# A graph layer on one core: zeroing two edge-count tables without waiting for the small constants

## The chip, the cores and the metric

The kernel runs on one core of one Trainium2 chip. Its time is the device time of one execution in microseconds (us); a kernel is judged by the median of several executions. Engines are called PE (matrix multiply), DVE (vector), ACT (scalar), POOL (GpSimd) and SP (the queue that issues most loads and stores). Transfers that SP issues and transfers that POOL issues run on the same 16 DMA engines, in two queues that the profile calls q1 (hardware, SP's) and q0 (software, POOL's).

## The reference, cut to what matters

```python
# x: 1250 nodes x 768; src, dst: 21250 edges (20000 and one loop per node)
xn = layernorm(x)
# graph branch: its edges are src -> dst and one more loop per node
e     = leaky_relu(s_src[src] + s_dst[dst])
alpha = softmax of e over the edges of one dst
out   = segment_sum(alpha * h[src], dst)          # twice: 4 heads of 192, then 2 heads of 96
# mix branch: k, q, v = xn @ kqv_w.T + kqv_b; exp features of k and q by mix_w; linear attention; projection
x = x + gnn(xn) + mix(xn)
# then a layer norm, 8 experts with top-2 routing, and the last sum
x = x + ffn(layernorm(x))
```

The graph branch needs, for every pair (source, destination), how many edges join them. The kernel keeps this as a count matrix of 1280 x 1280 16-bit numbers in device memory.

## The kernel before

Nodes are laid out in ten tiles of 128 rows. Every engine has its own program, written out by hand; they meet at semaphores, so the order on each engine is the order in the code.

**The count tables.** Two tables in device memory, `table[0]` and `table[1]`, each 1280 x 1280 and a small spill area (3201 KB), are zeroed by POOL with one transfer each from a zero tile in on-chip memory (line 538). Then, for 28 chunks of 6 columns of 128 edges, DVE compares each edge's key with those of its neighbours (`compare_chunk`, line 922, operations at lines 929 to 939) and POOL adds the counts into the tables with 168 indirect transfers (line 549), three to each table per chunk. The first of them waits for the zeroing of its table, and each waits for the chunk's slots (`slots_done`). Much later POOL reads both tables back (`cnt`, lines 561 and 565).

**POOL's start.** POOL fills the zero tile and some constants with memsets, waits until DVE has copied the transposed edge keys out of a PSUM bank (`keyT`), writes them to `key_d` with two transfers (lines 530 and 531), and then comes to the zeroing.

**SP's start.** In this order: the edges, x in tiles 0 to 5, half 0 of the k weights (`w_raw`, line 410), x tiles 6 to 9, then 31 small constants that all count on the semaphore `consts_in`: `kqb_c`; `gb_c` in two transfers of 4-byte pieces, 1536 in all (line 419); three rows of 3 KB broadcast to 128 partitions (`accb`, `row_t`, `row_b`, line 422); 24 pieces of `mix_w` of 64 partitions x 128 bytes (lines 426 and 428); the router weights (`rw_raw`, line 429, last, 768 pieces of 32 bytes). After them come half 1 of the k weights (line 410), the v weights (`whole`, line 408, 768 pieces of 3 KB) and the edge keys broadcast to all partitions (`keyrow`, line 438).

**Who waits for the constants.** `N_CONST` is 31, and four engines wait for all of them: PE ahead of its first k product (line 1321), ACT after it has cast half 1 of the k weights (line 640), DVE after it has split x (line 919), and POOL ahead of the zeroing (line 535).

**The stage around them.** DVE takes the mean and variance of x tile by tile (`tile_stats`, lines 876 to 880), normalises tiles 0 to 4 and then 5 to 9 (line 914); PE transposes each half (line 1291); ACT and DVE split the transposed halves into high and low parts. PE then runs 18 k groups in a row (`K_MAIN`, line 1280), and ACT evacuates each (lines 647 and 648). After the eleventh (`j == 10`) ACT takes a square root (`root(3)`, line 629) for which DVE waits after its first two compare chunks (line 869); only then does DVE do the other 26 chunks, and PE's first product over the values waits until they are done.

Of the kernel before, what the change touches and what calls it, by code (L numbers as in the profile page):

```python
# [22 lines left out]
def gps_layer(nc, x, src, dst, norm_g, norm_b, W1, a_src1, a_dst1, b1, W2, a_src2, a_dst2, b2, Wu, bu,  # L23
# [12 lines left out]
    H2, C2 = a_src2.shape  # L36
    MH, HD, M = mix_w.shape
    E, _, FI = w1T.shape
    GR = src.shape[1]
    KW = 3  # L40
# [15 lines left out]
    with ctx:  # L56
# [143 lines left out]
        def sem(name):  # L200
            return ctx.enter_context(nc.semaphore(name))
# [3 lines left out]
        consts_in, edges_in, rows_in = sem("consts_in"), sem("edges_in"), sem("rows_in")  # L205
# [187 lines left out]
        N_CONST = 7 + 2 * MH  # L393
# [111 lines left out]
        def _(pool):  # L505
# [26 lines left out]


            pool.wait_ge(zero_done, 1)
            pool.wait_ge(consts_in, 16 * N_CONST)
            for i, tab in enumerate(table):
                view = tab.rearrange("(p a n) o -> p a (n o)", p=P, n=ZW)
                pool.dma_start(view, zero[:, :].unsqueeze(1).broadcast_to([P, view.shape[1], ZW])).then_inc(table_zeroed[i], 16)
# [1092 lines left out]
```

## Time and profile before

| what | value |
|---|---|
| median of 3 runs | 1316.11 us (1314.32 to 1346.6) |
| the profiled execution's own time | 1314.55 us |
| its span, first to last instruction | 1312.8 us |
| PE, DVE, ACT, POOL busy | 83%, 62%, 31%, 23% of the span |
| chain that ended last, by engine | PE 60%, DVE 26%, issue 7%, DMA 3% |
| mean granted clock of PE | 0.916 |

Work in the profile is told by engine, line of the kernel and operands (out<-in). The chain that ended last is followed back from the last instruction; time outside it costs nothing by itself. Times within the execution are microseconds from the start of the span.

### The profile page before, as it was taken

Reading aid. Unit: us, or ns where it says so; the run is one execution under the profiler, and the core shown is the slowest. Engines: PE = TensorE matmul, PEld = TensorE weight load, DVE = VectorE, ACT = ScalarE, POOL = GpSimd, SP = SyncE. Lnnn points to the kernel's source line nnn. Section 1 sums busy time; section 2 is a strip of 40 time slices with the busy share of each in tenths; the row PEclk is TensorE's granted clock in tenths of the full one; section 3 lists DMA queues with packets and bytes.
Section 4 is the critical chain, followed back from the end, with each engine's and each line's share of the span. In section 5 each row is a group of like instructions: output and inputs, shape, how many; then the busy total and the mean of one; then the engine's idle time right before and its main releaser. Section 6 shows DMA issues by size and latency. Waiting matters only on the chain.

```text
span 1312.8 us, 15580 instructions
## 1 busy us (share of the span) xinstructions
PE 1092.2 (83%) x6105; PEld 975.1 (74%) x6105; DVE 816.8 (62%) x1648; ACT 401.0 (31%) x522; POOL 306.4 (23%) x227
## 2 busy tenths in 40 slices
PE   2999956999999992018999794678699999999998
PEld 1898535667899992018888794677569999999998
DVE  7558993107632595978999668697935433454344
ACT  2443010334100214017666331672242221222211
POOL 1157888888883400010000000000000000000000
PEclk8999985999999996558999897798899999999999
DMA  6926652423555804012000002001010111011103
GB/s 205 312 47 157 127 102 14 72 1 50 118 117 57 238 18 138 0 41 81 1 1 0 1 22 99 0 1 49 1 48 1 48 48 49 1 48 49 49 0 118
DMA packets 67241, 83.14 MB, mean 63 GB/s; under 512 B 31419, under 2 KB 50189, under 8 KB 67169
## 3 DMA queue, kind: packets, MB, share of 16 engines
q1 hardware_dynamic: 37601, 62.27, 15.2%
q0 software_dynamic: 29568, 19.89, 10.1%
q8 instruction: 48, 0.79, 0.3%
q14 instruction: 24, 0.20, 0.0%
HBM read 67.59 MB, written 14.54 MB: 63 GB/s over the span
## 4 chain that ended last, share of the span: by engine, by line
PE 60%; DVE 26%; issue 7%; DMA 3%; ACT 3%; POOL 1%; DVEq 0%; SPq 0%; ACTq 0%; POOLq 0%
PE bank L1280 51%; PE bank L1482 7%; DVE junk_m L1060 7%; DVE junk_k L929 6%; DVE pbuf L1131 3%; DVE pbuf L1105 3%; PE bank L1291 2%; ACT vbuf L762 1%; DVE h L1114 1%; DMA cnt<-table 1%; DVE sb_stats L876 1%; DVE x L1180 1%; DVE sb_stats L877 1%; ACT pbuf L771 1%; DMA keyrow<-key_d 1%
## 5 line engine op out<-in xcount | busy, mean ns | idle before, releaser
L549 POOL DMA_INDIRECT table<-match_n,slot_ix x168 | 277.6, 1652 | 89.6 <-issue 49.7
L1482 PE MATMUL bank<-h,pbuf 128*128 128x193 f32 (+1 forms) x1200 | 190.2, 319 | 31.5 <-DVE pbuf L1131 30.4
L1482 PEld LDWEIGHTS bank<-h,pbuf 128*128 128x128 f32 x1200 | 181.6, 197 | 40.1 <-DVE pbuf L1131 35.9
L1280 PE MATMUL bank<-f_hi,hT 128*128 128x384 f32 x640 | 167.4, 336 | 0.0
L1280 PEld LDWEIGHTS bank<-f_hi,hT 128*128 128x128 f32 x640 | 117.0, 189 | 0.6
L1211 DVE TENSOR_TENSOR hT<-silu,hT 128x512 fp32r<-128x512 f32 (+1 forms) x48 | 28.8, 603 | 141.4 <-ACT hT L825 141.3
L1262 DVE SCALAR_TENSOR_TENSOR x<-bank,sb_gate,x 128x384 f32<-128x384 f32 x160 | 93.5, 613 | 28.9 <-PE bank L1280 28.6
L1280 PE MATMUL bank<-f_lo,hT 128*128 128x384 f32 x320 | 107.7, 337 | 0.0
L1280 PE MATMUL bank<-y2T_hi,f_hi 128*128 128x512 f32 (+1 forms) x288 | 103.2, 358 | 2.9 <-DVE y2T_lo L860 2.9
L929 DVE SCALAR_TENSOR_TENSOR junk_k<-keyrow,key,sb_before 128x384 uint8<-128x384 f32 x168 | 92.8, 614 | 20.1 <-DMA keyrow<-key_d 20.1
L1280 PE MATMUL bank<-y2T_lo,f_hi 128*128 128x512 f32 (+1 forms) x288 | 102.9, 357 | 0.0
L1280 PE MATMUL bank<-y2T_hi,f_lo 128*128 128x512 f32 (+1 forms) x288 | 102.9, 357 | 0.0
L1060 DVE CUSTOM_DVE_ANT_0 junk_m<-a_row,pen 128x1280 bf16<-128x1280 f32 x60 | 89.5, 1492 | 21.1 <-DMA a_row<-s_d 12.2
L823 ACT ACTIVATE silu<-bank 128x512 f32<-128x512 f32 (+1 forms) x48 | 25.4, 528 | 244.9 <-PE bank L1280 244.9
L771 ACT ACTIVATE pbuf<-pbuf 128x1280 f32<-128x1280 f32 x60 | 76.1, 1269 | 58.3 <-DVE pbuf L1105 58.3
L1131 DVE SCALAR_TENSOR_TENSOR pbuf<-pbuf,cnt 128x1280 f32<-128x1280 f32 x60 | 88.7, 1484 | 0.0
L1280 PE MATMUL bank<-xnT_hi,w_hi 128*128 128x512 f32 (+1 forms) x216 | 84.4, 391 | 0.9 <-ACT qpT L674 0.9
L1280 PE MATMUL bank<-w_hi,xnT_hi 128*128 128x384 f32 x240 | 81.2, 338 | 0.0
L1280 PE MATMUL bank<-w_hi,xnT_lo 128*128 128x384 f32 x240 | 80.7, 336 | 0.0
L1280 PE MATMUL bank<-w_lo,xnT_hi 128*128 128x384 f32 x240 | 80.6, 336 | 0.0
L1280 PE MATMUL bank<-xnT_lo,w_hi 128*128 128x512 f32 (+1 forms) x216 | 77.8, 360 | 0.0
L1280 PE MATMUL bank<-xnT_hi,w_lo 128*128 128x512 f32 (+1 forms) x216 | 77.6, 359 | 0.0
(244 smaller groups left out, 1992.3 us busy)
## 6 DMA issues: line engine op xcount, KB each, us to landing
keyrow<-key_d SPq DMA_DIRECT2D x28, 384.0 KB
table<-zero POOLq DMA_DIRECT2D x2, 3201.0 KB, 28.4
cnt<-table POOLq DMA_DIRECT2D x20, 320.0 KB, 10.9
f_raw<-in_w1T SPq DMA_DIRECT2D x8, 768.0 KB, 4.8
f_raw<-in_w2T SPq DMA_DIRECT2D x8, 768.0 KB, 6.3
w_raw<-in_kqvT SPq DMA_DIRECT2D x4, 1152.0 KB, 7.1
acc_d<-ubuf SPq DMA_DIRECT2D x20, 192.0 KB, 2.1
u_row<-m_d POOLq DMA_DIRECT2D x6, 640.0 KB, 7.8
```

The costliest lines, as they stand in the source:

```text
L549: pool.indirect_dma_start(table[i], bass.IndirectOffsetOnAxis(ap=slot_ix[:, g:g + 1], axis=0), match_n[:, g:g + 1], None, compute_op=ALU.a ...
L771: nc.scalar.activation(pbuf[i % 3][:, :], pbuf[i % 3][:, :], ACT.Exp).then_inc(e_done, 1)
L823: nc.scalar.activation(sbuf[g % 3][:, 0:w], b[:, 0:w], ACT.Silu).then_inc(free("H", e, c, m), 1)
L929: nc.vector.scalar_tensor_tensor(out=junk_k[g % 2][:, :], in0=keyrow[c % KR][:, w:w + KW * P], scalar=key[:, g:g + 1], in1=before[:, first ...
L1060: ins = nc.vector.tensor_tensor_reduce(out=junk_m[:, :], in0=rows_a[h][:, :], in1=pen_t[:, :], scale=1.0, scalar=-3e38, op0=ALU.subtract, ...
L1105: nc.vector.scalar_tensor_tensor(out=pbuf[i % 3][:, :], in0=u1_r[h][:, :], scalar=scol[:, h, st:st + 1], in1=vbuf[i % 2][:, :], op0=ALU.ad ...
L1131: nc.vector.scalar_tensor_tensor(out=pbuf[i % 3][:, :], in0=pbuf[i % 3][:, :], scalar=2.0, in1=cnt[st][:, :], op0=ALU.min, op1=ALU.mult).t ...
L1211: nc.vector.tensor_tensor(hT[j % 2][1][:, g % 2, 0:w], sbuf[g % 3][:, 0:w], hT[j % 2][0][:, g % 2, 0:w].bitcast(F32), ALU.subtract).then_i ...
L1262: nc.vector.scalar_tensor_tensor(out=a, in0=b[:, 0:HALF], scalar=gate[:, t, e:e + 1], in1=a, op0=ALU.mult, op1=ALU.add).then_inc(free("O", ...
L1280: return nc.tensor.matmul(o, l, r, start=first, stop=last)
L1291: ins = nc.tensor.transpose(b[0:channels, j * P:(j + 1) * P], piece(j), ident[:, :])
L1482: ins = nc.tensor.matmul(b[:, d * stride:d * stride + chans + 1], score[:, dt * P:(dt + 1) * P], h_t[:, st, h, 0:chans + 1], start=st == 0 ...
```

## The change

One wait is taken out of POOL's program. The zeroing of the two tables then waits only for the zero tile; the two key transfers still stand ahead of it, and every reader of the tables keeps its wait.

```diff
@@ -532,7 +532,6 @@
             pool.wait_ge(zero_done, 1)
-            pool.wait_ge(consts_in, 16 * N_CONST)
             for i, tab in enumerate(table):
                 view = tab.rearrange("(p a n) o -> p a (n o)", p=P, n=ZW)
                 pool.dma_start(view, zero[:, :].unsqueeze(1).broadcast_to([P, view.shape[1], ZW])).then_inc(table_zeroed[i], 16)
```

No instruction changes its place on any engine. POOL's list around the zeroing, with what each instruction waits for, was this before (`key_d` is the key scratch, `zero` the zero tile):

```order
L530 DMA key_d<-keyT 128x128 [waits bank_free0,consts_done]
L531 DMA key_d<-keyT 40x128
L538 DMA table<-zero 1536x1x1067 [waits consts_in,zero_done]
L538 DMA table<-zero 1536x1x1067
L549 DMA table<-match_n,slot_ix 1638912x1 [waits table_zeroed0,slots_done]
```

and is this with the change (the lines behind it are numbered one less):

```order
L530 DMA key_d<-keyT 128x128 [waits bank_free0,consts_done]
L531 DMA key_d<-keyT 40x128
L537 DMA table<-zero 1536x1x1067 [waits zero_done]
L537 DMA table<-zero 1536x1x1067
L548 DMA table<-match_n,slot_ix 1638912x1 [waits table_zeroed0,slots_done]
```

The zeroing follows the key transfers at once, and nothing else moves.

## Rows read from the trace of the kernel before

**Rows 1.** The chain of waits in order of time: start us, us, what.

```profile
38.72 23.34 PE bank L1280 x125
...
91.99 0.69 ACT kq L647
...
94.65 0.22 ACT sb_sq L629
...
96.05 3.34 DVE junk_k L929 x12
```

**Rows 2.** Who waited for whom, whole span: us in total, times, longest us.

```profile
POOL table L538 <- DMA sb_rw_raw<-in_routerT: 27.7, 1, 27.7
...
POOL cnt L561 <- DMA acc_d<-ubuf: 25.7, 1, 25.7
...
DVE junk_k L929 <- DMA keyrow<-key_d: 20.1, 4, 15.3
...
DVE sb_rs L869 <- ACT sb_sq L629: 14.4, 4, 13.6
```

**Rows 3.** Timeline of POOL: start us, us, engine, line, operation, idle before it.

```profile
8.33 0.58 POOL L531 DMA_DIRECT2D key_d<-keyT  x1
36.64 2.05 POOL L538 DMA_DIRECT2D table<-zero  x2 [27.74 <-DMA sb_rw_raw<-in_routerT]
```

**Rows 4.** Timeline of SP's DMA queue: start us, us taken to issue.

```profile
9.81 4.29 SPq L419 DMA_DIRECT2D sb_gb_c<-in_norm_b  x1
14.13 2.59 SPq L422 DMA_DIRECT2D sb_accb<-in_bu  x1
...
18.56 0.55 SPq L426 DMA_DIRECT2D sb_wk<-in_mix_w  x1
...
33.87 0.59 SPq L429 DMA_DIRECT2D sb_rw_raw<-in_routerT  x1
34.50 0.55 SPq L410 DMA_DIRECT2D w_raw<-in_kqvT  x1
```

**Rows 5.** DMA issues by line: KB each, median us from issue to landing.

```profile
sb_rw_raw<-in_routerT SPq DMA_DIRECT2D x1, 24.0 KB, 2.2
```

**Rows 6.** Timeline of DVE, PE and ACT, one row of each.

```profile
28.70 0.56 DVE L876 BATCH_NORM_STATS2 sb_stats<-xrow 128x6 f32<-128x384 f32 x1
...
38.51 0.47 PE L1280 MATMUL bank<-xnT_hi,w_hi 128*128 128x512 f32 x1
...
40.70 2.13 ACT L601 ACTIVATE w_hi<-w_raw 128x2304 fp32r<-128x2304 f32 x1 [1.40 <-DMA w_raw<-in_kqvT]
```

**Rows 7.** DMA packets of 0 to 13.6 us, all queues, by size.

```profile
DMA packets 2057, 3.98 MB, mean 293 GB/s; under 512 B 177, under 2 KB 1213, under 8 KB 2057
```

**Rows 8.** DMA queues, 13.6 to 23 us: packets, MB, share of 16 engines.

```profile
q1 hardware_dynamic: 3072, 2.63, 99.4%
```

**Rows 9.** DMA queues, 36 to 41 us (no row of q0 there).

```profile
q1 hardware_dynamic: 899, 1.57, 96.4%
```

**Rows 10.** DMA queues, 42 to 57 us.

```profile
q0 software_dynamic: 770, 3.25, 58.2%
q1 hardware_dynamic: 798, 2.35, 44.2%
```

**Rows 11.** DMA queues, 60 to 63 us.

```profile
q0 software_dynamic: 215, 0.92, 102.9%
```

**Rows 12.** DMA queues, 63 to 66 us.

```profile
q0 software_dynamic: 137, 0.58, 105.6%
```

**Rows 13.** DMA queues, 113.5 to 118.5 us.

```profile
q1 hardware_dynamic: 622, 1.83, 98.6%
q0 software_dynamic: 515, 0.00, 16.1%
```

**Rows 14.** Stretches: us, busy time of each engine (instructions), PEclk, DMA share, GB/s.

```profile
24.60:32.20 7.60, 0.00 (x0) 0.00 (x0) 6.84 (x21) 2.00 (x2) 0.00 (x0) 0.50 0.09 14
32.20:38.20 6.00, 6.00 (x27) 5.63 (x28) 6.00 (x8) 4.16 (x9) 1.56 (x2) 0.50 0.49 115
```

## The prediction, made before the changed kernel had run

> **What bounds the kernel now.** I read the chain of waits first, then the list of waits, then the timelines of the queues around the edit, and last what the DMA queues moved.
>
> The chain says who sets the pace at the start. PE enters it with the k products at 38.7 us; it leads through PE's work to ACT's evacuation at 91.99 and the square root at 94.65, and hands over to DVE's compare chunks at 96.05, on which the next PE stage hangs [rows 1]. So a shift of the first k product is a shift of everything behind it, and a shift of DVE's first two chunks alone is not: after them DVE stood 13.6 us waiting for that square root [rows 2].
>
> The count tables are off this chain. POOL waited 27.7 us for the last constant before it zeroed [rows 2, 3], but after its last scatter it stood 25.7 us waiting for something else [rows 2]. POOL's scatters of chunks 2 to 27 need DVE's slots, which come only after 96 us [rows 1]. Zeroing earlier by itself therefore buys nothing.
>
> **What the change does, part by part.**
>
> *The wait.* The issue of the zeroing moves from 36.64 to just behind the key transfer that ends at 8.91 [rows 3], 27.7 us earlier. Before, no packet of q0 moved from 36 to 41 [rows 9]; by 42 to 57 they ran at full rate [rows 10]. That is 4.4 to 5.4 us from issue to the first packet; I take 4.7, so zeros begin to move at about 13.6.
>
> *What they meet there.* 2057 packets had moved by 13.6, 1213 of them under 2 KB [rows 7]. The other 844, less 16 of the keys, are rows of x, so of its 1280 rows about 450 are still to come. Behind them in SP's queue stand 1664 small pieces (`kqb_c` 128, `gb_c` 1536), 384 rows of 3 KB, 24 pieces of `mix_w` and the router weights. Before, SP's queue had the engines alone: 3072 packets from 13.6 to 23 at 99.4% [rows 8]. After that they were nearly idle while SP issued its small transfers, and that is the gap that invites the change.
>
> *How the two queues share.* From 42 to 57 q0 moved 770 packets of zeros and q1 798 of loads [rows 10], one for one, 51 pairs a us. The zeros are some 1540 packets (two tables of 3201 KB, at the 4.2 KB a packet of this row). Do small pieces pair one for one too? The nearest rows: at 113.5 to 118.5, 2-byte scatter packets and 3 KB loads ran 515 to 622 [rows 13]. I take one for one, as these rows are near to it.
>
> *The sum for the constants.* (1) 450 x rows at 51 pairs a us: 8.8 us, so x is in at about 22.4. DVE needs the last tile at 28.70 [rows 6]; covered, with 6 us left, and without that cover a late tile would push DVE, then PE's transposes, one for one. (2) The 1090 zeros left pair with the small pieces at the rate of zeros alone: 215 in 3 us, 72 a us [rows 11], gives 15.1 us, to 37.5. At the slower rate of the row behind it, 46 a us [rows 12], it would be 23.7 us, to 46. (3) SP cannot run far ahead of its queue: the second transfer of `gb_c` took 4.29 us to issue and the next 2.59, against 0.55 to 0.59 once the queue had drained [rows 4]. When the 4.29 ended, the packets issued and not moved were 450 less those of half a us, and 1664: some 2000 to 2100, and I take 2048 as what fits. Three rows then go out as x drains, by 22; after that each `mix_w` transfer of 64 pieces waits for 64 to drain. 1090 drained pieces let 17 of the 25 last transfers out by 37.5. The 8 left take 0.64 us each (25 in the 15.9 us from 18.56 to 34.50 [rows 4]), 5.1 us, to 42.6, and the last lands 2.2 us after its issue begins [rows 5]: about 44. The 384 rows (1.2 MB) need some 3.5 us of the same stretch and are hidden in it.
>
> *What hangs on it.* PE starts its k products at 44 and not at 38.51 [rows 6]: **+5.5 us**. POOL's other user of the semaphore is gone; DVE's sum at line 920 waits too, but its next work, the first compare chunk, waits for `keyrow` anyway (15.3 us before [rows 2]). ACT's cast of half 1, issued 0.6 us behind the last constant, moves from 40.70 to about 49; its product is used after two k groups, some 8.5 us after 44, so it just fits. `keyrow` lands behind it and the v weights, at about 56 (57.8 before), with 13.6 us and more of cover.
>
> *PE's clock.* PE had no work from 24.6 to 32.2 and its granted clock was 0.50, the 1.2 GHz level; it stayed there for 6 us of work, to 38.2 [rows 14]. With the change PE stands from 38.5 to 44; no row shows an idle stretch of just that length, so it may fall again or not. If it is low for the first 5 us or so of the k products, they lose half of these: **+2.5 us**, between 0 and 3; I take the fall, since the stretch that is shown is the nearest.
>
> *The other side of the ledger.* From 42 to 72 the loads no longer share with zeros. What they feed there is `keyrow`, whose wait lies under the 13.6 us: 0. The scatters lose their wait for the second table (3 us of POOL): 0 under the 25.7.
>
> Sum: 5.5 + 2.5 = **+8 us** on the profiled execution's 1314.55, 1322.6. The median stands 1.6 above that execution, and it is of three runs with one far off; I say **1323 us**.
>
> **The Trainium skill against this.** The Trainium skill, "DMA: Bandwidth & Descriptors", section on queues, rings and completion order, says that each DMA engine alternates between queues by packets, and that such a packet is typically 9 to 17 descriptors. By that rule small pieces would pass in bundles and the constants would be late by rival A's amount, not by mine; the trace's 515 to 622 is of single 2-byte elements and speaks against it weakly. The same section says that a completion increment lands only after every earlier write of its DMA engine, in whatever queue, which speaks against this change; no run here shows it, and it would add to the lateness.
>
> **The rivals.**
>
> *A, small pieces pass in bundles.* Then the 1664 pieces cost about a us; x ends at 22.4 instead of 18, the 384 rows pair with zeros (7.5 us) but only hold back pieces behind them. SP's `mix_w` issues start about 4 us late, at 22.5, and the last constant lands at 22.5 + 15.9 - 0.6 + 2.2 = 40. PE: +1.5, and its clock may not fall: +1.5 to +4, **1317 us**. For it: four-byte pieces moved very fast before (3072 packets in 9.4 us with 2.6 MB, [rows 8]). Against it: rows 10 and 13.
>
> *B, the constants are in by 38.5 all the same: not slower.* Before, they were in at 36.64, 1.9 us before PE asked [rows 3, 6]. If SP's issues are not held by the queue (the 4.29 and 2.59 being the cost of making 4-byte pieces, not a full queue), SP is done at 34.5 as before and the small pieces only need to drain by 38.5. This decides the sign: a lateness under 1.9 us costs nothing. Time **1314.5 us**, between -2 and +1. For it: the engines were idle from 23 to 36. Against it: by (1) and (2) zeros alone fill them to 37.5.
>
> *C, the slow rate holds throughout.* Zeros to 46, seven transfers left to issue, constants at about 52: +14, and +3 of clock: **1332 us**. For it: [rows 12]; against it: that row is a tail, and the rates before it are higher.
>
> *D, the zeroing does not start early.* Nothing else holds it: the zero tile is filled in the first 2 us. 1 in 100.
>
> **How the numbers follow.** Forecast (+5 to +12) 0.46; A 0.24; B 0.19; C 0.09; D 0.01; over +26 us 0.01. The range takes in A and B and the lower part of C: **1314 to 1330 us**. About 2% (26 us) is what a measurement of this kernel can tell from no change; every case but the last lies inside it: faster 0.01, within 2% 0.97, slower 0.02.
>
> **What would show it.** In the changed kernel's profile: the zeroing issued at about 8.9; `mix_w` issues that take more than 0.6 us each, and the last constant issued near 42 (step 3; at 34 to 35 it is B, near 38 A); the first k product at about 44, and PEclk at 0.5 in the first us behind it; x statistics without a wait for x (step 1); `junk_k` starting near 56 and DVE's wait for the square root grown to about 20 us; POOL's wait before `cnt` still about 25. The forecast is wrong in kind if PE starts at 38.5, or if x tiles arrive late.

## The result, and the profile after

| | kernel before | changed kernel |
|---|---|---|
| median of 6 runs, taken together | 1317.45 us (1314.31 to 1347.41) | 1345.95 us (1328.53 to 1362.84) |
| ratio to the kernel before | | 1.0109, 95% interval 1.0077 to 1.0141 |

In both kernels some executions take about 30 us more than the others: the ratios and single times given here and below leave them out, and of the profiles taken in one of them (1359.19 us here, and those of runs 2, 7 and 9) only the first 450 us are read, in which this one agrees within 3 us with that of run 1, the same kernel again. With the change the times are 1328.53, 1329.5 and 1332.71 us, before 1314.31 to 1318.79: the change costs about 14 us, 1.1%. The forecast was +8, and 1323 us.

The chain of waits at its start (start us, us, what; engine "SPq" is SP's DMA queue), against [rows 1]:

```profile
9.90 11.22 SPq L419
21.16 11.47 SPq L422
32.67 1.58 SPq L422
...
50.65 2.18 DMA sb_rw_raw<-in_routerT
...
52.87 55.10 PE bank L1279 x318
```

and the same view where PE hands over to DVE:

```profile
108.00 0.70 ACT kq L646
...
110.66 0.22 ACT sb_sq L628
112.06 3.34 DVE junk_k L928 x12
```

Before, the chain entered this stage with PE's own work. Now it comes through SP's queue: two issues of 11 us each. PE's first k product moved from 38.51 [rows 6] to 52.87, 14.4 us; the square root from 94.65 [rows 1] to 110.66, 16.0 us. The stage behind it passes most of that on: the load of `cnt` begins at 443.96, before at 431.64.

The list of waits, first of the whole span, then of the first 120 us (us in total, times, longest us), against [rows 2]:

```profile
POOL cnt L560 <- DMA acc_d<-ubuf: 21.9, 1, 21.9
...
DVE sb_rs L868 <- ACT sb_sq L628: 23.1, 4, 22.2
```

```profile
PE bank L1279 <- DMA sb_rw_raw<-in_routerT: 14.0, 1, 14.0
```

PE has a wait that it did not have before, 14.0 us for the last constant. DVE's wait for the square root grew from 13.6 to 22.2 us. POOL's wait before `cnt` is 21.9 us, where it was 25.7: it is shorter by 3.8 us, and the tables are still far from the chain.

POOL's timeline and that of SP's queue (start us, us taken to issue), against [rows 3, 4]:

```profile
8.86 2.09 POOL L537 DMA_DIRECT2D table<-zero  x2
```

```profile
9.90 11.22 SPq L419 DMA_DIRECT2D sb_gb_c<-in_norm_b  x1
21.16 11.47 SPq L422 DMA_DIRECT2D sb_accb<-in_bu  x1
32.67 1.58 SPq L422 DMA_DIRECT2D sb_row_t<-in_proj_b  x1
34.29 0.48 SPq L422 DMA_DIRECT2D sb_row_b<-in_v_b  x1
34.81 0.54 SPq L426 DMA_DIRECT2D sb_wk<-in_mix_w  x1
35.40 0.59 SPq L428 DMA_DIRECT2D sb_wq<-in_mix_w  x1
...
50.65 0.59 SPq L429 DMA_DIRECT2D sb_rw_raw<-in_routerT  x1
```

The zeroing starts at 8.86, as meant. The same two SP issues that took 4.29 and 2.59 us take 11.22 and 11.47, and the first piece of `mix_w` is issued at 34.81 instead of 18.56. From there to the router weights the 24 pieces take 15.8 us, 0.5 us more than before (18.56 to 33.87). So nearly all of the delay, 16.3 of 16.8 us, arose in front of them.

What the DMA queues moved, first from 14 to 21 us and then from 26 to 36 (packets, MB, share of 16 engines):

```profile
q0 software_dynamic: 393, 1.68, 61.3%
q1 hardware_dynamic: 400, 1.07, 41.2%
```

```profile
q0 software_dynamic: 642, 2.71, 99.2%
q1 hardware_dynamic: 641, 0.00, 6.6%
```

Both are one for one. In the first stretch q1's packets are mostly rows of x, in the second they are 4-byte pieces, which before had passed with the x rows at 3072 in 9.4 us [rows 8]. Now 641 take 10 us, as many as the 4.2 KB packets of zeros that pass with them. q1 has 6.6% of the engines and next to no bytes, and it is still what everybody waits for. The same view from 34 to 37, and from 37 to 40:

```profile
q0 software_dynamic: 175, 0.75, 103.3%
q1 hardware_dynamic: 177, 0.00, 7.4%
```

```profile
q0 software_dynamic: 82, 0.29, 58.2%
q1 hardware_dynamic: 672, 0.13, 57.4%
```

The zeros thin out behind 37 (40 packets in the first of these 3 us, then 26 and 16), and as soon as they do, q1 moves 672 packets in 3 us.

Last the stretches around PE's start (us, busy time of PE, PEld, DVE, ACT, POOL with their instructions, PEclk, DMA share, GB/s), against [rows 14]:

```profile
41.00:52.80 11.80, 0.00 (x0) 0.00 (x0) 0.94 (x3) 0.00 (x0) 0.00 (x0) 0.58 0.37 92
52.80:56.00 3.20, 3.13 (x7) 2.48 (x8) 0.96 (x1) 0.00 (x0) 0.00 (x0) 0.50 0.92 311
56.00:60.00 4.00, 4.00 (x18) 3.19 (x17) 0.00 (x0) 2.51 (x2) 0.00 (x0) 0.94 1.04 405
```

After the idle stretch PE runs its first 3.2 us at 0.50, the 1.2 GHz level, and is back at 0.94 in the next 4 us. From the first product to the evacuation it takes 55.1 us, before 53.5 (38.51 to 91.99): 1.6 us more, as much as 3.2 us at half the clock lose.

### The profile page after: what moved, and what is told of

Its sections match the earlier page's. It is cut to its first block, busy times and chain, and to the rows that moved or that the text cites. A ratio compares the mean times of both kernels' runs of the same rounds, so it can differ in the third digit from the quotient of the medians.

```text
span 1357.4 us, 15579 instructions
## 1 busy us (share of the span) xinstructions
PE 1122.6 (83%) x6105; PEld 1004.0 (74%) x6105; DVE 817.5 (60%) x1648; ACT 401.8 (30%) x522; POOL 306.1 (23%) x227
## 4 chain that ended last, share of the span: by engine, by line
PE 60%; DVE 24%; issue 6%; SPq 4%; DMA 3%; ACT 2%; POOL 1%; DVEq 0%; ACTq 0%; POOLq 0%
PE bank L1279 51%; PE bank L1481 7%; DVE junk_m L1059 7%; DVE junk_k L928 6%; DVE pbuf L1130 3%; DVE pbuf L1104 3%; PE bank L1290 1%; SPq L422 1%; ACT vbuf L761 1%; DVE h L1113 1%; DMA cnt<-table 1%; SPq L419 1%; DVE x L1179 1%; ACT pbuf L770 1%; DMA keyrow<-key_d 1%
## 5 line engine op out<-in xcount | busy, mean ns | idle before, releaser
L1481 PEld LDWEIGHTS bank<-h,pbuf 128*128 128x128 f32 x1200 | 184.3, 200 | 38.9 <-DVE pbuf L1130 34.8
```

Of the source, the lines that this page charges most:

```text
L1481: ins = nc.tensor.matmul(b[:, d * stride:d * stride + chans + 1], score[:, dt * P:(dt + 1) * P], h_t[:, st, h, 0:chans + 1], start=st == 0 ...
```

## The experiments

The theory: PE's late start is the loss, and it is late because SP's issues are held while its small pieces share the engines with zeros, one for one. The rivals were the zeros' bandwidth, the tables themselves, and the `mix_w` pieces. In all runs below three marks are read: the first k product, the square root and the start of the `cnt` load, given as the difference to before (38.51, 94.65 and 431.64 us). Two profiles of the changed kernel differ by up to 2.8 us in them. No ratio stands where there were too few times for one.

**1. The changed kernel again.** No edit.

> The changed kernel once more, for its own times and a second profile. Both theories: first k product at 52.9 us against 38.5 before, total 1329 us, 14 us over the kernel before; the DVE compare chunks behind the square root start 14 to 16 us later.

Marks +15.2, +16.8, +15.2 us; times 1329.23, 1331.64, 1333.42; ratio 1.0108 (1.0068 to 1.0149). The result holds, and the first 450 us account for all of it.

**2. The 4-byte loads out of the way.** The changed kernel with both `gb_c` loads behind the second `keyrow` load, on a semaphore of their own that only their readers wait for (`N_CONST` is lowered to match).

```diff
-            for j, v in enumerate((norm_g, norm_b)):
-                sp.dma_start(gb_c[:, j, :], v.rearrange("o (k p) -> p (o k)", p=P), ...).then_inc(consts_in, 16)
...
+                if c == 1:
+                    for j, v in enumerate((norm_g, norm_b)):
+                        sp.dma_start(gb_c[:, j, :], v.rearrange("o (k p) -> p (o k)", p=P), ...).then_inc(gb_in, 16)
```

> The changed kernel, with the two transfers of 4-byte pieces (gb_c) moved behind the second keyrow load, on a semaphore of their own. Pairing theory (a packet of zeros passes between each two pieces of SP's queue, whatever their size, and SP's issues are held behind the 4-byte pieces): no issue of SP takes over 3 us, the first mix_w transfer is issued near 22 us (34.8 in the changed kernel), the first k product starts at 40 to 45, total 1317 to 1321 us. Bandwidth theory (the 6.5 MB of zeros delay the constants by their bytes): the moved pieces are 6 KB, so nothing improves: first k product at 50 or later, total 1327 us or more.

Marks +7.5, +10.2, +10.3; the one time is 1320.9, inside what was expected, and PE's start at 46.0 is just behind it. So 1536 pieces in front of the rest cost about half of the lateness of PE's start and a third of the other two marks'. The bandwidth theory, by which 6 KB less could not help, falls. SP's queue shows why it is not all (start us, us to issue):

```profile
12.39 2.18 SPq L424 DMA_DIRECT2D sb_wk<-in_mix_w  x1
...
16.79 2.22 SPq L426 DMA_DIRECT2D sb_wq<-in_mix_w  x1
19.05 0.63 SPq L424 DMA_DIRECT2D sb_wk<-in_mix_w  x1
...
40.53 0.59 SPq L427 DMA_DIRECT2D sb_rw_raw<-in_routerT  x1
```

The first piece of `mix_w` is issued at 12.39 (22 was expected), before even the time of the old kernel, but many issues now take 1 to 2.6 us, and the last constant still goes out at 40.53. The hold moved to the next small transfers.

**3. One table early.** The second table waits for the constants again, as both did before.

```diff
             for i, tab in enumerate(table):
+                if i == 1:
+                    pool.wait_ge(consts_in, 16 * N_CONST)
```

> The changed kernel with only the first table zeroed early; the second waits for the constants as before. Pairing theory: the 770 packets of zeros are gone near 27 us, mix_w begins near 28, the last constant is issued near 44, first k product at 46, total 1322 to 1325. Bandwidth theory: half the bytes, half the loss: first k product at 45 to 46, total 1321 to 1323. Both are alike here; it measures the dose.

Marks +6.2, +7.9, +5.9; times 1319.98 and 1324.66. Half of the zeros, about half of the loss; both theories had said so. SP's queue:

```profile
9.52 11.91 SPq L419 DMA_DIRECT2D sb_gb_c<-in_norm_b  x1
21.47 2.03 SPq L422 DMA_DIRECT2D sb_accb<-in_bu  x1
...
26.61 0.78 SPq L426 DMA_DIRECT2D sb_wk<-in_mix_w  x1
...
42.38 0.59 SPq L429 DMA_DIRECT2D sb_rw_raw<-in_routerT  x1
```

The first issue is held as long as with two tables (11.91); the second, 11.47 there, is back to 2.03. With half the zeros the hold is over sooner.

**4. The zeroing between the small pieces and `mix_w`.** The kernel before, but its zeroing waits for the three rows alone; they are given a semaphore of their own, for which PE and DVE wait as well.

```diff
-                sp.dma_start(r[:, :], v.broadcast_to([P, D])).then_inc(consts_in, 16)
+                sp.dma_start(r[:, :], v.broadcast_to([P, D])).then_inc(rows6_in, 16)
...
-            pool.wait_ge(consts_in, 16 * N_CONST)
+            pool.wait_ge(rows6_in, 16 * 3)
```

> The kernel before, but the zeroing waits only for the three broadcast rows (in at about 23 us), so zeros move from about 27.7 us beside nothing but mix_w and the router weights: some 1470 pieces of 128 and 32 bytes, 0.1 MB. Pairing theory: these pieces go one for one with zeros at about 72 a us, so the router weights land at 45 to 48 and the first k product starts at 45 to 48, total 1323 to 1327. Bandwidth theory: 0.1 MB is nothing beside idle engines, SP issues as before, first k product at 38.5 to 39.5, total 1314 to 1316.

Marks +12.1, +14.0, +13.4; 1327.77 to 1332.86; ratio 1.0118 (1.0091 to 1.0144). As bad as the change itself, with all 4-byte pieces and all of x out of the way. It is worse than the pairing theory expected (PE's start at 50.6, not 45 to 48), and the bandwidth theory (38.5 to 39.5) is excluded. SP's queue, then what moved from 28 to 43 us:

```profile
25.08 0.60 SPq L427 DMA_DIRECT2D sb_wk<-in_mix_w  x1
25.72 1.42 SPq L429 DMA_DIRECT2D sb_wq<-in_mix_w  x1
27.18 1.57 SPq L427 DMA_DIRECT2D sb_wk<-in_mix_w  x1
...
43.92 0.59 SPq L430 DMA_DIRECT2D sb_rw_raw<-in_routerT  x1
```

```profile
q0 software_dynamic: 1151, 4.84, 98.9%
q1 hardware_dynamic: 719, 0.07, 5.2%
```

The zeroing is issued at 24.01, and from 25.72 on a transfer of 64 pieces takes about 1.4 us to issue, 0.60 before. So the last constant is issued 10.0 us later than before (12 such issues with 0.8 us more each, and one with 0.3); its landing takes 6.7 us instead of 2.2 [rows 5], another 4.5, and some 2 us of slack come off. q1 moved 0.07 MB in 15 us, so the loads lack no bandwidth. Nor is it one for one here, 719 to 1151: beside zeros at 77 a us, 64 pieces with a turn each would pass in 0.8 us, and an issue took 1.4. The 4-byte pieces had been issued long before, and the issues were held all the same.

**5. PE's wait for the constants put off.** In the changed kernel PE waits for them only ahead of its second k group.

```diff
-            pe.wait_ge(consts_in, 16 * N_CONST)
...
+                if j == 1:
+                    pe.wait_ge(consts_in, 16 * N_CONST)
```

> The changed kernel with PE's wait for the constants moved from ahead of the first k product to ahead of the second one (the first that needs a result made with them comes behind it). If the loss is PE standing for the constants and nothing else, the first group of 18 products runs at 38.5, before the wait, and 4.3 us of the 14 come back: total 1324 to 1326. If DVE's or ACT's later data set the pace instead (half 1 of the weights lands at 57.5), nothing comes back: 1329.

First product at 38.33, marks +12.9 and +12.9 for the other two; ratio 1.0104 (1.004 to 1.0168). PE's wait is down to 9.4 us, and the square root comes 3.8 us sooner than in run 1, where one k group had been to gain (4.3 expected); the `cnt` mark gains 2.3. The times (1325.54 to 1337.61, 1324 to 1326 expected) cannot be told from those of the changed kernel. By the mark, what PE does while it waits comes off the loss. The rival has a part too: the chain here no longer runs through the last constant but through half 1 of the k weights, which SP issues behind it (50.48, landed 5.9 us later) and whose cast ACT does before it evacuates the first k group. So a shorter wait for the constants would have met that load next; it was not tried. The chain there:

```profile
50.48 5.92 DMA w_raw<-in_kqvT
...
58.45 0.68 ACT kq L646
...
59.83 2.28 PE bank L1279 x17
```

**6. Is the square root the hand-over?** The kernel before, with the square root after the ninth k group.

```diff
-                if j == 10:
+                if j == 8:
                     root(3)
```

> The kernel before, with the square root that DVE waits for taken two k groups earlier on ACT (after the ninth, at about 82 us and not at 94.6). If DVE's chain behind that root sets the pace, as the chain of waits says, all of it moves by 10 to 11 us: total 1304. If PE or POOL set the pace there, nothing moves: 1315.

Marks: root -10.7, `cnt` -11.4; the one time is 1303.96, where 1304 was expected. The chain's claim, that DVE's work behind this square root sets the pace, is borne out: the `cnt` mark, and in this one time the end, move with the root.

**7. Fewer `mix_w` transfers.** The changed kernel with the 24 in six, the same data.

```diff
-            for h in range(MH):
...
+            by_half = mix_w.rearrange("(k q) i m -> q i k m", q=2)
+            by_pair = mix_w.rearrange("(j a q) i m -> a q i j m", a=2, q=2)
+            for q in range(2):
+                r = slice(HD * q, HD * (q + 1))
+                sp.dma_start(wk[r, :, M * q:M * (q + 1)], by_half[q]).then_inc(consts_in, 16)
+                for a in range(2):
+                    f0 = 64 * a + M * q
+                    sp.dma_start(wq[r, a:KD:2, f0:f0 + M], by_pair[a, q]).then_inc(consts_in, 16)
```

> The changed kernel with the same pieces of mix_w in 6 transfers instead of 24. If SP's issuing behind the held queue is the last part of the lateness (24 transfers of 0.6 us from 34.8 on), the router weights are issued near 40 and the first k product starts at 42 to 45, total 1318 to 1321. If it is the number of pieces that pass beside zeros, this changes nothing, since the pieces are the same: first k product at 50 or later, 1327 to 1329.

Marks +8.5, +10.6, +10.3; 1326.96 to 1328.37; ratio 1.0083 (1.0057 to 1.011). The first `mix_w` issue is at 34.09, as in the changed kernel, and the last constant at 42.29 instead of 50.65. The 0.6 us of issue that each of the 24 costs is thus a real part of the delay once it can no longer lie under PE's transposes. PE's start, 47.0, lies between what the two theories expected (42 to 45, and 50 or later); the time is the one expected if only the number of pieces counts (1327 to 1329), and the ratio's interval overlaps that of run 1. So the marks show that the issues have a part, and that they are not all; in the time their part is not clear of noise.

**8. Both, on the kernel before.** The late zeroing, `mix_w` in six as in run 7, and the square root after the sixth k group.

```diff
-                if j == 10:
+                if j == 5:
                     root(3)
```

> The kernel before, zeroing late, with mix_w in 6 transfers and the square root taken after the sixth k group. The constants are in near 26, so zeros start there and keyrow is issued near 24 and is in before DVE asks at 42.5; DVE's two compare chunks and statistics end near 66, the root is taken at 72, 22 us earlier than before. PE had 25 us of idle time there. Total 1293 to 1297. If zeros from 30 on hold back keyrow or half 1 of the weights, less: 1300.

Marks 38.38 (the same), -21.0, -21.0; 1292.8, 1295.97 and 1301.27; ratio 0.9849 (0.9791 to 0.9907). It beats both kernels. The chain of waits, the queue and the list of waits:

```profile
38.44 32.52 PE bank L1283 x172
...
73.64 0.22 ACT sb_sq L632
75.05 3.33 DVE junk_k L932 x12
```

```profile
22.82 0.60 SPq L432 DMA_DIRECT2D sb_rw_raw<-in_routerT  x1
```

```profile
25.67 2.05 POOL L541 DMA_DIRECT2D table<-zero  x2 [16.79 <-DMA sb_rw_raw<-in_routerT]
```

```profile
DVE junk_k L932 <- DMA keyrow<-key_d: 7.9, 3, 4.0
```

With six transfers the constants are out at 22.82, and the zeroing, which still waits for them, starts at 25.67: 11 us earlier than before, and PE's start is unmoved: with the constants in by 25.67, they are not what it waits for. The gain goes with the square root, as in run 6; the earlier `keyrow` (its wait is 4.0 us, before 15.3) would keep DVE ready for it. How much of the 21 us the six transfers give was not tried: no run moves the root to the sixth group alone.

**9. The early zeroing on top of run 8.** The wait is taken out there too.

> Kernel e8 (mix_w in 6 transfers, the root after the sixth k group), now with the zeroing at the very beginning as in the changed kernel. If the early zeroing costs the same wherever the root is taken, as long as PE stands for the constants: first k product at 47 as in e7, root at 81 against 73.6 in e8, total 1303 to 1307 against 1297. If it is the gain of an earlier keyrow that counts now, as the old slack is used up: no slower than e8, 1297 or less.

Against run 8: first product +8.1, root +10.3, `cnt` +10.5; 1301.69 to 1311.56; ratio to the kernel before 0.9929 (0.9904 to 0.9955), 0.8% above run 8's. PE's start (46.4) is as expected (47), the root (83.9, not 81) later. The change costs the same kind of thing on a kernel that is better prepared for it.

**10. Run 9 with the 4-byte loads behind `keyrow`,** as in run 2.

> Kernel e9, and the 4-byte pieces of gb_c moved behind keyrow as in e2: the version in which early zeros should meet least. Pairing theory: 450 rows of x, 384 rows of constants and some 700 pieces of mix_w each take a packet of zeros with them, so the constants are in at 40 to 42; first k product at 40 to 43, root at 74 to 77, total 1297 to 1301, still not better than e8. Rival, that the 4-byte pieces were all there was to it: first k product at 38.5, root at 72, total 1295 or less.

Against run 8: +4.8, +7.2, +7.0; 1300.47 to 1304.22; ratio to the kernel before 0.9889 (0.9868 to 0.9911). PE's start (43.2) and the root (80.8) come later even than the pairing theory's 40 to 43 and 74 to 77, and the rival (38.5 and 72) falls. What moved from 23 to 37 us:

```profile
q0 software_dynamic: 795, 3.32, 72.7%
q1 hardware_dynamic: 791, 1.28, 30.7%
```

Once more one for one. Even with the pieces most exposed to it gone, zeroing early is no better than zeroing when the constants are in: its marks are later than run 8's, and the intervals of the two ratios overlap. PE stood only 4.5 us here, and still its first 3.9 us of work ran at a granted clock of 0.50.

## Why the prediction was wrong

The sign was right, and so were the path and the pairing; how long SP's issues are held was not, and with it the size: +14 us against +8, with PE's start +14.4 against +5.5 and the clock +1.6 against +2.5.

- **Zeroing early buys nothing.** Right: POOL's wait before `cnt` was 21.9 us in the changed kernel, and between 21.9 and 25.8 in every run.
- **Sum, step 1, x in time.** Right. 400 packets against 393 from 14 to 21, 57 pairs a us for my 51, and DVE's last tile at 29.02 with no wait for x (28.70 before).
- **Step 2, small pieces pair one for one.** Right in kind, 641 against 642. The rate was 64 pairs a us and not 72 from 26 to 36, and the zeros thinned out from 37 on, the last of them at about 40 (predicted 37.5). The last 4-byte load, issued at 9.90, landed 31.6 us later, at 41.5.
- **Step 3, what SP issues meanwhile.** This is the step that failed. I had the three rows out by 22 and 17 of the last 25 transfers out by 37.5; in fact the rows were held to 34.8, and only 5 of the 25 had been issued at 37.5. The last constant was issued at 50.65 and not 42.6. The model behind it was a queue that holds 2048 packets and lets SP on when they drain. The packets counted leave no such size. By that model the issue that began at 9.90 ends when as many of q1's packets have passed as before, 86 from 13.6 to 14.13; here 452 had passed by 21.16, when the next one began. That one had ended when 549 had passed (at 16.74), here when 1225 had (at 32.67). So of the 450 rows of x and 1664 small pieces about 1700 were outstanding when `accb`'s issue began at 21.16, and with its own 128 rows about 1000 when SP was let on. In runs 2 and 4 issues were held too (1 to 2.65 and 1.4 us for 0.60) with the 4-byte pieces behind them or gone.
- **The 0.6 us per `mix_w` transfer.** I took them to go out beside the drain. They came after the hold, 15.8 us in a row, 15.3 before. So the 16.3 us by which the first of them was late reached the last constant whole (16.8); run 7, with six of them, got 6 of the 14 us of PE's start back.
- **ACT's cast of half 1 just fits.** Right in kind: it came at 57.49 (I had about 49), and the chain shows no break in PE's work. `keyrow` was later than I said, DVE's first compare chunk at 65.36 and not 56, and its cover held: DVE then still waited 22.2 us for the square root.
- **The clock.** It did fall, as taken: 0.50 for the first 3.2 us, and 1.6 us lost, not 2.5. The wait was 14.0 us, not the 5.5 for which I had no row; run 10 has 0.50 behind one of 4.5 us.
- **The rivals.** A (bundles) falls by 641 to 642; C had PE's start right, +14, and a total close to the measured one, +17, by luck: it needed a rate of 46 a us until 46, which no stretch of the load shows. B and D fall with the timelines. My range stopped at 1330, in the middle of the measured times, because I gave the lateness of the constants one cause and bounded it by the zeros' rate alone; the issue had no upper bound in my sum though [rows 4] showed it at 4.29 us.

The Trainium skill, "DMA: Bandwidth & Descriptors", section on queues, rings and completion order, lets an engine drain a packet of typically 9 to 17 descriptors before it turns to the other queue. The trace disagrees as far as its rows count packets: 641 four-byte rows in q1 to 642 of 4.2 KB in q0.

**What stays open** is what exactly holds SP's issue. It ends earlier when the zeros do (run 3), it takes 64-piece transfers as well as 768-piece ones (runs 2, 4), and it is not bytes (run 4). But in the changed kernel the issues from 34.8 to 38 took 0.60 us although zeros still moved, 175 from 34 to 37. No single size of the queue (above) and no fixed price of an issue fits all of these. A kernel with zeros in larger or smaller packets would tell; it wasn't tried.

## What to carry to other kernels

A transfer that is off the critical path is not free to start when the engines look idle: the share that a small load gets beside a bulk store goes by packets, so ask how many pieces, and not how many bytes, the loads beside it have, and whose start waits for the last of them. Before moving bulk work forward, get the many-piece loads out first and in few transfers; in this kernel six transfers in the place of 24 let the zeroing start 11 us sooner with PE's start unmoved (run 8), while zeroing both tables at 8.9 us made PE's start at least 4.8 us late in every arrangement in which it waited for the constants. And read the chain for the hand-over: one square root taken two k groups earlier gave 11 us (run 6), and five groups earlier, with the six transfers, 21 us (run 8).

## What the runs showed of the hardware that was not expected

- Two queues that both had packets waiting shared the engines one packet for one packet: 642 of 4.2 KB to 641 of 4 bytes in 10 us, and 795 to 791 beside larger loads. Where SP's issues were the limit, they did not (1151 to 719, run 4).
- The issue of a transfer with many small pieces is held beside a bulk store from the other queue: 4.29 to 11.22 us and 2.59 to 11.47 us for 768-piece and 128-row transfers, 0.60 to 1.4 us for 64 pieces. A load of 3 KB in 4-byte pieces took 31.6 us to land, before 10.0.
- After waits of 4.5 us (run 10) and 14 us PE's first 3 to 4 us of work had a granted clock of 0.50, the 1.2 GHz level; in the next 4 us it was 0.83 and 0.94.
